# A two-layer convolution and spectral kernel: order of the TensorE work in a turn, the type of the scaled chunk, and the length of the ring

## What is computed

```
x1 = x + L0(gn(x))          x: (8, 32, 512, 512) float32
out = x1 + L1(gn(x1))       gn: 16 groups of 2 channels, per image

L0: s = max|t|; q = clip(round(t*127/s), -127, 127)   # activations and weights
    3x3 convolution of integers, padding 1, times sx*sw/127^2, plus bias
L1: rfft2(ortho), 32 x 16 lowest modes, einsum with complex R (32 x 32 channels), irfft2
```

## Time and profile before

| | |
|---|---|
| median of three runs | 3662.15 us (3650.08 to 3663.09) |
| profiled execution, its own time | 3657.67 us |
| its span | 3655.8 us |
| PE, DVE, ACT, POOL busy | 84%, 88%, 65%, 23% of the span |
| DMA | 1352.55 MB, mean 370 GB/s |
| second stage | about 660 to 2300 us of the span |

### The profile page before, as it was taken

One profiled execution on the slowest core, in us unless ns is written; L12 is line 12 of the kernel. 1 busy time (PEld: TensorE's weight loads), 2 busy tenths in 40 slices (PEclk: granted clock), 3 DMA queues, 4 the chain that ended last, 5 costly groups with the idle time before them and its releaser, 6 DMA issues.

```text
span 3655.8 us, 81588 instructions
## 1 busy us (share of the span) xinstructions
PE 3067.9 (84%) x33145; PEld 1535.0 (42%) x33145; DVE 3219.5 (88%) x3272; ACT 2379.1 (65%) x3507; POOL 825.1 (23%) x1040
## 2 busy tenths in 40 slices
PE   5666666699999999999999999788888888888886
PEld 1111111366666666666666666433222222222222
DVE  6999999999899999999898999399888888888887
ACT  6888888688888888889888888443333333333332
POOL 0000000255454455555454545000000000000000
PEclk7777778799999999999999999799999999999998
DMA  9999999899999999999999999489999999999998
GB/s 398 421 421 421 421 421 421 246 352 350 316 343 333 323 335 331 343 326 351 307 350 320 335 333 313 160 339 427 427 427 427 427 427 426 422 420 420 422 420 373
DMA packets 342541, 1352.55 MB, mean 370 GB/s; under 512 B 45792, under 2 KB 47040, under 8 KB 243808
## 3 DMA queue, kind: packets, MB, share of 16 engines
q1 hardware_dynamic: 223104, 811.13, 60.9%
q0 software_dynamic: 82272, 268.58, 20.2%
q10 hardware_dynamic: 36864, 268.45, 17.4%
HBM read 811.10 MB, written 536.87 MB: 369 GB/s over the span
## 4 chain that ended last, share of the span: by engine, by line
DMA 43%; DVE 25%; PE 22%; issue 5%; ACT 3%; SPq 1%; DVEq 0%; POOL 0%; ACTq 0%
DMA out<-ring 20%; DMA ring<-x_scratch 10%; DVE ring L574 9%; PE ps L725 8%; DMA ring<-in_x 8%; PE ps L736 6%; DVE area L556 5%; DVE area L551 3%; DVE area L560 3%; ACT area L315 2%; DMA vbuf<-in_x 2%; PE ps L746 2%; DVE ring L662 2%; PE ps L687 2%; DMA mixb<-in_x 2%
## 5 line engine op out<-in xcount | busy, mean ns | idle before, releaser
L291 POOL DMA_DIRECT2D x_scratch<-ring x1024 | 819.1, 807 | 1474.5 <-DVE ring L574 1451.7
L872 PE MATMUL ps<-x,gj_s 128*128 128x512 bf16 x3072 | 773.3, 406 | 215.7 <-DVE ring L662 214.7
L725 PE MATMUL ps<-area,wq 128*32 128x512 bf16 x12264 | 765.7, 383 | 36.0 <-DVE ring L574 16.1
L662 DVE TENSOR_TENSOR ring<-ps,ring 128x1024 f32<-128x1024 f32 x512 | 602.9, 1219 | 163.3 <-DMA ring<-x_scratch 161.2
L574 DVE SCALAR_TENSOR_TENSOR ring<-ps,sc,ring 128x1024 f32<-128x1024 f32 x512 | 637.2, 1279 | 74.3 <-PE ps L725 67.2
L340 ACT ACTIVATE area<-ps 128x512 f32<-128x512 f32 x1024 | 555.5, 599 | 131.1 <-PE ps L736 130.2
L872 PEld LDWEIGHTS ps<-x,gj_s 128*128 128x128 bf16 x3072 | 294.6, 103 | 772.1 <-DVE ring L662 440.7
L736 PE MATMUL ps<-id_s,ring 128*128 128x128 f32 x4096 | 562.0, 280 | 15.6 <-ACT area L340 10.5
L479 DVE TENSOR_REDUCE stat<-area 128x1 f32<-128x4096 f32 x128 | 559.3, 4411 | 12.4 <-ACT area L315 12.0
L347 ACT ACTIVATE area<-ring,qtab 128x2048 bf16<-128x2048 f32 x256 | 513.6, 2006 | 0.0
L736 PEld LDWEIGHTS ps<-id_s,ring 128*128 128x128 f32 x4096 | 444.3, 141 | 163.5 <-issue 112.4
(11 more groups left out here) (135 smaller groups left out, 2209.9 us busy)
## 6 DMA issues: line engine op xcount, KB each, us to landing
ring<-in_x SPq DMA_DIRECT2D x1024, 256.0 KB, 6.8
x_scratch<-ring POOLq DMA_DIRECT2D x1024, 256.0 KB, 6.7
ring<-x_scratch SPq DMA_DIRECT2D x256, 1024.0 KB, 12.3
out<-ring ACTq DMA_DIRECT2D x256, 1024.0 KB, 24.7
ring<-in_x SPq DMA_DIRECT2D x148, 1024.0 KB, 20.6
vbuf<-in_x SPq DMA_DIRECT2D x36, 1024.0 KB, 21.1
mixb<-in_x SPq DMA_DIRECT2D x36, 1024.0 KB, 21.2
x<-in_x SPq DMA_DIRECT2D x36, 1024.0 KB, 21.1
```

What stands on the lines that cost most here:

```text
L291: pool.dma_start(x1_rows[b, m, r], xslot(t % SL)[32 * r:32 * r + 32, :].rearrange("p (g w) -> p g w", g=4)).then_inc(s_x_out[t % SL], 16)
L662: nc.vector.tensor_tensor(half, ps[0][:, hj * 2 * HW:(hj + 1) * 2 * HW], half, ALU.add).then_inc(s_add, 1)
L725: last = mm(ps[0][32 * cg:32 * cg + 32, HW * g:HW * g + HW], wq[:, (3 * a + dw) * C:(3 * a + dw + 1) * C], src[:, 1 + dw:1 + dw + HW], sta ...
L872: last = mm(bank(j), gj_s[:, (j * 3 + v) * 128:(j * 3 + v + 1) * 128], (z12, z12, z13)[v][:, k % 2], start=(v == 0), stop=(v == 2))
```

## The change

The four parts:

1. PE: a turn runs `turn_x1` v=0, 1, then both halves of the convolution, then `turn_x1` v=2, 3, then `along_w1`. Before, v=2, 3 stood between the two halves. The first `turn_rows` of a turn moves from behind the first half to ahead of it.
2. `u` is a tile of 16-bit integers: the write of `u` by ACT and DVE rounds, and the rounding step becomes a plain conversion from int16 to bf16.
3. The ring has 9 slots instead of 8. The ninth can be loaded before the loop starts, without a wait of its own.
4. What follows: `area` is smaller, the tiles in it move, R is loaded to slots 4 to 7 and waits for the chunks that were last in these, and the third stage uses slots 0 to 7 as they stand.

```diff
-        ring = sb("ring", [128, SL * FC])
-        area = sb("area", [128, 16 * WP + 3 * FC - FC // 2 + 2 * FC])
+        ring = sb("ring", [128, XS * FC])
+        area = sb("area", [128, GT * 64])
...
-        u = area[:, 2 * qn:2 * qn + 2 * FC].rearrange("p (s f) -> p s f", s=2)
+        u = area[:, 2 * qn:2 * qn + FC].bitcast(I16).rearrange("p (s f) -> p s f", s=2)
...
-            for t in range(SL):
-                if t % 2 == 0:
+            for t in range(XS):
+                if t < 8 and t % 2 == 0:
                     sp.wait_ge(s_sq, max(n for n in range(NT) if n % NGS == t // 2) + 1)
                 load(t)
-            for t in range(T):
-                if t and t + 7 < T:
-                    sp.wait_ge(s_x_out[(t - 1) % SL], ((t - 1) // SL + 1) * 64)
-                    sp.wait_ge(s_t, 4 * t)
-                    sp.wait_ge(s_ss, t)
-                    load(t + 7)
+            for t in range(1, T - XS + 1):
+                sp.wait_ge(s_x_out[(t - 1) % XS], ((t - 1) // XS + 1) * 64)
+                sp.wait_ge(s_t, 4 * t)
+                sp.wait_ge(s_ss, t)
+                load(t + XS - 1)
...
-                nc.vector.tensor_scalar(q[:, g0:g0 + 4, 2:2 + HW], u[:, t % 2].rearrange("p (g w) -> p g w", g=4),
-                                        MAGIC, MAGIC, ALU.add, ALU.subtract).then_inc(s_r, 1)
+                nc.vector.tensor_copy(q[:, g0:g0 + 4, 2:2 + HW],
+                                      u[:, t % 2].rearrange("p (g w) -> p g w", g=4)).then_inc(s_r, 1)
...
                     turn_x1(i - 4, 0)
                     turn_x1(i - 4, 1)
+                if small and j < 4:
+                    turn_rows(b, 2 * j)
                 if 2 <= i and i - 2 < T:
                     conv(i - 2, 0)
-                if small and j < 4:
-                    turn_rows(b, 2 * j)
+                    conv(i - 2, 1)
                 if 4 <= i and i - 4 < T:
                     turn_x1(i - 4, 2)
                     turn_x1(i - 4, 3)
-                if 2 <= i and i - 2 < T:
-                    conv(i - 2, 1)
```

More of the change, by code:

```diff
@@ L7 @@
 BF16 = mybir.dt.bfloat16
+I16 = mybir.dt.int16
 ALU = mybir.AluOpType
@@ L34, in build @@
     SL = 8
+    XS = 9
     TB = NCH
@@ L168, in build @@
         s_wl = sem("weights_landed")
-        s_x_in = [sem(f"chunk_landed{k}") for k in range(SL)]
-        s_x_out = [sem(f"chunk_stored{k}") for k in range(SL)]
+        s_x_in = [sem(f"chunk_landed{k}") for k in range(XS)]
+        s_x_out = [sem(f"chunk_stored{k}") for k in range(XS)]
         s_u = sem("scaled_done")
@@ L236, in load @@
                 for r in range(4):
-                    sp.dma_start(xslot(t % SL)[32 * r:32 * r + 32, :].rearrange("p (g w) -> p g w", g=4),
-                                 x_rows[b, m, r]).then_inc(s_x_in[t % SL], 16)
-            for t in range(SL):
-                if t % 2 == 0:
+                    sp.dma_start(xslot(t % XS)[32 * r:32 * r + 32, :].rearrange("p (g w) -> p g w", g=4),
+                                 x_rows[b, m, r]).then_inc(s_x_in[t % XS], 16)
+            for t in range(XS):
+                if t < 8 and t % 2 == 0:
                     sp.wait_ge(s_sq, max(n for n in range(NT) if n % NGS == t // 2) + 1)
                 load(t)
-            for t in range(T):
-                if t and t + 7 < T:
-                    sp.wait_ge(s_x_out[(t - 1) % SL], ((t - 1) // SL + 1) * 64)
-                    sp.wait_ge(s_t, 4 * t)
-                    sp.wait_ge(s_ss, t)
-                    load(t + 7)
[L251 to L257, removed]
+            for t in range(1, T - XS + 1):
[3 more added lines that the diff above has]
+                load(t + XS - 1)
+            for k in range(4, 8):
+                sp.wait_ge(s_x_out[k], len(range(k, T, XS)) * 64)
+            last = max(t for t in range(T) if 4 <= t % XS < 8)
+            sp.wait_ge(s_t, 4 * (last + 1))
+            sp.wait_ge(s_ss, last + 1)
+            sp.dma_start(ring[:, 4 * FC:8 * FC], rt).then_inc(s_rl, 16)
+            for k in (0, 1, 2, 3, 8):
+                sp.wait_ge(s_x_out[k], len(range(k, T, XS)) * 64)
             sp.wait_ge(s_t, 4 * T)
@@ L328, in scaled @@
                 b = t // TB
[L329 removed]
+                act.wait_ge(s_x_in[t % XS], (t // XS + 1) * 64)
                 if t >= 2:
                     act.wait_ge(s_r, t - 1)
[L332 removed]
+                act.activation(u[:, t % 2, 0:HF], xslot(t % XS)[:, 0:HF], ACT.Identity,
                                bias=qtab[:, 2 * B + b:2 * B + b + 1],
@@ L346, in squared @@
                     act.wait_ge(s_dc, b - 1)
-                act.activation(junk_q, xslot(t % SL), ACT.Square, bias=qtab[:, 3 * B + b:3 * B + b + 1],
+                act.activation(junk_q, xslot(t % XS), ACT.Square, bias=qtab[:, 3 * B + b:3 * B + b + 1],
                                accum_out=ssq[:, (b % 2) * TB + m:(b % 2) * TB + m + 1]).then_inc(s_ss, 1)
@@ L572, in combine @@
                 dve.wait_ge(s_conv, 2 * t + h + 1)
-                half = xslot(t % SL)[:, h * HF:(h + 1) * HF]
+                half = xslot(t % XS)[:, h * HF:(h + 1) * HF]
                 nc.vector.scalar_tensor_tensor(out=half, in0=ps[0][:, h * HF:(h + 1) * HF], scalar=col(26), in1=half,
```

22 lines of the change are left out of this document (11 added, 11 removed).

## The result

The changed kernel takes 3622.97 us (median, 3620.56 to 3625.82) against 3662.62 for the former kernel beside it: ratio 0.9907, 95% interval 0.989 to 0.9925. Measured a second time, the ratio is 0.9903 (0.9887 to 0.992). The forecast was 3622 us. The profiled execution took 3620.56 us with a span of 3618.7, against 3657.67 and 3655.8.

The account below looks back on a forecast made before the run. DVE bound plain turns at 5.92 us, PE those after an image's end; with PE bounding everywhere, 5.6 + 31.7 = 37.3 us off 3657.67 gave 3620.4, stated as 3622 for the median, range 3596 to 3654.

Parts of the forecast that it names:

- DVE, the conversion at 0.69 us, a DVE turn of 5.38: Second stage, DVE: int16 conversion takes 0.69 us instead of the rounding's 1.23, so a turn falls from 5.92 to 5.38.
- PE bounds, 5.75 us a turn, the order saves nothing: Second stage: with faster DVE, PE bounds everywhere; both orders change weight shape equally often, so its turn stays 5.75 us.
- the order does save: Rival, PE in the second stage: joining the convolution halves spares 0.10 us more a turn, 25 us, giving 3596; chance 0.11.
- The late copies: Second transpose group comes later, so ACT frees its banks later, still 0.7 us before PE wants them; cost 0.
- The tight place: `turn_rows` ahead of the convolution waits for `rows_copied`, ready at 7.65, wanted at 7.75 us; taken as 0, at most 14.
- The ninth slot: Ring of loads: removes no work, asks for loads a turn earlier; costed at nothing, but without it part of the gain goes.
- The image, 199.1 us: Second stage: one image's PE work 198.6 us plus 0.5 for DVE's turn with `spectrum`, against 203.7 before, 4.6 less.
- the forecast sum of 37.3: Whole gain in us: 5.6 from 33 plain turns ahead of the first spectrum, 31.7 from 6.9 images at 4.6.
- The 1.3 us for the two blocks behind the combinations: PE, once an image: the two blocks behind the combinations take 3.7 us instead of 1.0 + 1.4, so 1.3 more.
- DMA holds the turn: Rival, second stage: slow transfers keep the turn at about 5.9 us, only waits around the spectrum shrink, about 3653; chance 0.19.
- The conversion is no faster: Rival, DVE: the conversion takes 1.23 us, the turn stays 5.92 and nothing changes, about 3660 us; chance 0.05.
- integers lose the fast rate: Rival, DVE: a 16-bit conversion takes 2.4 us, the turn 7.1, 187 us more in all, 3849; chance 0.06.

Follow-up runs that it names:

- split_w1: Changed kernel with `along_w1` cut in two halves, one ahead of the last four transposes of the turn and one behind; 3706.72 us.
- order_only: Former kernel with the new order of PE alone, 8 slots and the old rounding; ratio 0.9997 to the former kernel.
- float_9: Changed kernel with fp32 `u` and the former rounding, so new order and nine slots are left; ratio 0.9962 to the former kernel.
- i16_order_8: Changed kernel with 8 slots instead of 9; ratio 0.9959 to the former kernel.
- i16_only: Former kernel with 16-bit integers alone, 8 slots and the former order of PE; 3647.29 us, ratio 0.9959 to the former kernel.
- conv_third_9: Changed kernel, 9 slots, with only the middle of the convolution's three taps along w computed (another function); 3550.66 us.
- oldorder_again: Changed kernel with the former order of PE, integers and nine slots kept, measured another time; 3624.33 us, ratio 0.9899 to the former kernel.

## Why the prediction was right, point by point

- **DVE, the conversion at 0.69 us, a DVE turn of 5.38.** Measured 0.69 and 5.39, the latter where PE does not hold it. Writing integers at nothing: `L553` 0.80, and on ACT `L334` stays at 1.24. Right.
- **PE bounds, 5.75 us a turn, the order saves nothing.** 5.77, or 5.75 in the former order, 0.9997 for the order alone. The mechanism, weight shapes and not types, is shown by split_w1. The rival "the order does save" is out.
- **The late copies.** Room for 0.7 us was given; PE's wait for ACT ahead of its transposes is 4.6 us in the whole stage. The tight place, `turn_rows` ahead of the convolution, was named and taken as 0, with 14 us at most. This term was too small, and the copy was another: `rows_copied`, which the prediction reckoned, is never waited for in the changed kernel; `w_copied`, which the first `turn_rows` of an image needs, is, seven times. With what follows that costs about 0.5 us an image, and the six turns from 5 on sum to 300.0 us where the former order has 294.1, 6 us more.
- **The ninth slot, "I cost it at nothing".** This step failed in part. It rested on "ACT's waits for loads cost nothing today: DVE runs without a gap while they happen". They cost: through ACT's queue they held PE (18.0 us in order_only, 2.5 in float_9), above all ahead of the first `turn_rows` (10.2 us against 2.2), which took from it the lead that absorbs this work, and twice over where the clock fell behind the wait. float_9 is 13 us faster than order_only, its interval clear of it. The other half of the statement, that a part of the gain goes without the slot, holds, but it is more than half: 15 us remain of some 36 (i16_order_8, i16_only). The sum came out right since it was made with PE as the bound everywhere, that is with the slot's work included.
- **The image, 199.1 us.** 198.2, and the forecast sum of 37.3 against 37.1 in the span. That the two sums agree this closely is in part luck: the terms inside moved more than that. By the turns of seven images: the seven turns around `turn_rows` cost 48.6 us an image against 46.9 before (before, PE's lead absorbed part, now PE pays it all), the seven behind them 41.3 against 42.6, the spectrum turn and the one after it 17.7 against 18.4, the eight behind 44.5 against 47.5. DVE catches up at 5.39 to 5.5 for three to six turns after each spectrum, about 2 us an image, which I had not counted. Against that stand turns of 5.77 for 5.75 and 4.6 us for the work of `turn_rows` instead of 4.0. The 1.3 us for the two blocks behind the combinations came from one image in which the clock was halved: the granted clock is 0.55 there in 981 to 983 us and 0.60 in 983 to 985. The trace of the kernel before has this in four images of seven, that of the changed kernel in two. No row gave the 0.9 us for single products and the 0.5 us for DVE's turn with `spectrum`; the turns were not split so far as to measure them.
- **DMA holds the turn** (0.19). Wrong at 5.77 us: waits for loads fell to 12.4 us. But in the first image turns reach 7.3 us, about 5 us in sum over 5.77 each, and ACT waits for loads there; and conv_third_9 does not keep its 5.39 us. The Trainium skill, page "DMA: Bandwidth & Descriptors", section "Bandwidth", says that the HBM side binds transfers between HBM and SBUF at about 358 GB/s, and gives that as a core's share when both cores of the pair stream. It is no bound for this one core: 362 in 700 to 850 us of the changed kernel, 376 in conv_third_9, 425 in the third stage.
- **The conversion is no faster; integers lose the fast rate.** Both excluded by 0.69 us.

## What to carry to other kernels

Where the bounding engine shows no gap, waits elsewhere may still cost: follow the wait down its engine's queue (load, scaled half, copy, PSUM bank, transposes), since what it takes is the lead of a near-critical engine, and that lead pays for the next burst of extra work. If that engine is PE, look at the granted clock behind the wait too. When two engines are within a few per cent, as DVE 5.92 and PE 5.75 here, speeding one up needs the buffers to go with it: integers alone gave 15 us, a slot alone 13, both about 36. And a long stall cut in pieces gives back only what the other engine did not catch up afterwards: 26.9 us in its own turns, 4.2 in all turns of the stage, and a time that its partner's range still overlaps.

## What the runs showed that I had not expected

- In the combinations, some hundred small matmuls in a row, PE stands without a wait that the profile shows, 1.2 to 4.4 us (the longest in i16_only); seven equal images of one execution have spectrum turns from 8.01 to 13.68 us. Cut in pieces they are 6.90 to 8.66, with one 12.65 in the turn behind. The cause stays open.
- A longer stand of PE costs twice. Behind PE's wait of 2.02 us in order_only and its stall of 3.25 us in oldorder_again the granted clock was 0.50; behind the wait of 0.32 us in float_9 it was not. From the 20th chunk to the last, the clock was at 0.50 for 13.7 us in the kernel before, 10.2 in the changed one, 23.9 in i16_only and 85.3 in conv_third_9.
- DMA's busy share is 1.01 to 1.04 at 342 GB/s as at 376 and 425: it does not show what is left.
- A conversion of 16-bit integers to bf16 on DVE is as fast as a bf16 copy, 0.69 us for 128x2048; fp32 to int16 is as fast as fp32 to fp32, 0.80 for 128x1024.
